# Attention over a graph on one core: one fp32 one-hot in a ring of five batches instead of two, the steps of PE, ScalarE and VectorE in another order, and the node numbers read as long runs

## The chip, the cores and the metric

The kernel runs on one core of a Trainium2 chip. The metric is the device time of one execution in microseconds (us). Before the change the median of three runs is 2317.58 us (2315.75 to 2317.67).

## What is computed

3,125 nodes carry 128 numbers each; 53,125 edges, sorted by their destination node, go from a node `src` to a node `dst`. Four layers follow one another, each with a residual and a layer norm: three sum messages over the edges, and the last is attention over them, in 8 heads of 16 numbers:

```python
q = (h @ Wq + bq).reshape(n, OUT_DIM, H) * scaling
k = (h @ Wk + bk).reshape(n, OUT_DIM, H)
v = (h @ Wv + bv).reshape(n, OUT_DIM, H)
s = jnp.einsum('edh,edh->eh', q[row], k[col])
m = jax.ops.segment_max(s, row, num_segments=n)
p = jnp.exp(s - m[row])
z = jax.ops.segment_sum(p, row, num_segments=n)
out = jax.ops.segment_sum((p / z[row])[:, None, :] * v[col], row, num_segments=n)
```

Here `row` is `src` and `col` is `dst`. The edges come in both directions (each drawn pair twice, and a loop for each node), and the kernel groups edges by `dst` and gathers keys and values by `src`, which gives the same sums.

## The kernel before, in words

The edges are cut into 416 chunks of 128 (one edge for each partition). The three sum layers take up the first 1,640 us or so; GpSimd (POOL) fetches the rows of each chunk with an indirect DMA, VectorE (DVE) makes one-hot factors, TensorE (PE) multiplies. The change touches none of that. It touches two stages behind it.

**The stage between the layers** (`post_body` in `sum_layers`). A loop of 15 turns, `u` = 0 to 14, over pairs of the 25 node tiles. DVE does in each turn `last_front(u)` (bias, residual, statistics), `keys_values(u - 2)`, `last_back(u)` (normalise), and then small tables for the attention: `row_tables` in turns 1 to 7 and `chunk_tables` (line 1165), two in each of the turns 3 to 8 and one in turn 9. `chunk_tables` compares each edge's node with its neighbour's. It reads `dT`, in which partition `c * 8 + head` holds the node numbers of chunk `c` of each of the 26 batches, 130 numbers a batch. POOL loads `dT` with 16 DMAs (line 540), one for each `c`: 26 pieces of 130 numbers, out of the array `flat`, to each of 8 partitions. The first `chunk_tables` waits until all 16 have landed. ScalarE (ACT) turns each pair of tables into penalties (line 788) in its own turns 5 to 12, and the rest behind the loop. SyncE (SP) stores keys and values to memory; when they are there, POOL may begin with the gathers of attention.

**Attention** (`attention`). POOL gathers keys and values of one chunk after another (line 1418, 416 gathers), into a ring of 64 chunks. The others work in batches of 16 chunks; a batch has four parts `q` of 4 chunks. Step `k` of the loop (`STEPS`, -1 to 28) has three batches in work: `k` ("now": its scores), `k-1` ("mid": its maxima and weights), `k-2` ("old": its sums), and prepares `k+1` ("nxt"). In a step each engine has its orders written out by hand, and each engine works them off in that order. The orders that matter:

- PE: `window_sums(q)` (lines 1485 and 1488) is the sum of the weighted values of 4 chunks into a window of 40 nodes: 8 fp32 products of `PV` with the one-hot `S01`, and 8 small ones. `queries(q)` (1448) spreads the queries of a window over 4 chunks of edges. `one_hot_rows(q)` (1438) turns the one-hot over, for the queries of the next batch. `scores_t`, `rows`, `columns`, `weights_back`, `difference` belong to the running maxima and the weights. `output_t` turns over a finished tile of nodes.
- DVE: `products(q)` (1684) multiplies queries with gathered keys: it waits for `queries(q)` and for the gathers. `head_part` (1690) sums them by head. `chunk_max` and `segment_max` scan for the maxima (1701, 1702), `row_max` (1715 to 1722) carries them over the chunks. `values(q)` (1751) weighs the gathered values into `PV`, a ring of two, so that `values(q)` waits until PE is through with `window_sums(q - 2)`. `add(q)` (1778) adds a window's sums. `one_hots(k)` (1677) makes the bf16 one-hot `oh1` of a batch with 4 instructions, and `window_factors(k)` (1738) makes the same one-hot again in fp32, as `S01`, with 4 more. `outputs(t)` and `normalise(t)` finish a tile.
- ACT: `rows_copy`, `rows_ordered`, `columns_copy` (1572 to 1589) move maxima about between PE and DVE. `deviation` (1609) needs its own function table, `weights` (1593, the exponential) another, so each is preceded by a table load. `thrice(q)` (1561) spreads `oh1` for `one_hot_rows(q)`, `one_hot_copy(q)` (1568) takes its result out of PSUM.

25 of the steps have a tile to finish (`outputs`), a few have none.

## Time and profile before

| | |
|---|---|
| median of 3 runs | 2317.58 us |
| the profiled execution | 2318.64 us, with a span of 2316.4 us |
| busy over the span: PE / DVE / ACT / POOL | 70% / 66% / 19% / 71% |
| sum layers | to about 1640 us |
| stage between | 1640 to 1733 us |
| gathers of attention | 1709.6 to 2266.1 us |
| steps of attention | 1735 to 2316 us |

The span is that of the instructions; 2.2 us of the execution lie around it. Matmuls are pipelined and their ends are modelled, so PE's busy share is not a share of its peak. A wait is put down to the last of the events it waited for.

### The profile page before, as it was taken

The numbers are of one execution on the slowest core, as the hardware profiler recorded it, in microseconds if no ns is written. First come the engines' busy times: TensorE is split into PE (matmuls) and PEld (weight loads), VectorE is DVE, ScalarE is ACT, GpSimd is POOL, SyncE is SP. The second block draws the span as 40 slices with busy tenths as digits, with TensorE's granted clock in tenths as the row PEclk, the third lists the DMA queues.
The fourth block names the chain that finished last, engine by engine and source line by source line (L and its number), as shares of the span: only waits on it lengthen the run. The fifth ranks groups of instructions, "written<-read, shape, count | busy, mean of one in ns | idle before, by whom it ended". The sixth has DMA issues, their size and how long they took to land.

```text
span 2316.4 us, 31992 instructions
## 1 busy us (share of the span) xinstructions
PE 1620.7 (70%) x8464; PEld 1228.6 (53%) x8464; DVE 1527.4 (66%) x5213; ACT 430.7 (19%) x906; POOL 1639.1 (71%) x1687
## 2 busy tenths in 40 slices
PE   4877777774767666765576656767547888888886
PEld 3555555553545544544444444444335767777775
DVE  8776766665656665665355555555667787788785
ACT  0000000002000000002011111111154443344342
POOL 6777777775777777775777777776237777777771
PEclk9755555555565666666567777777775555555555
DMA  5233233232233233234223233233444333333330
GB/s 139 56 84 85 56 84 86 56 85 73 55 84 85 84 85 112 57 84 143 67 84 98 84 99 98 84 99 93 67 128 114 108 105 108 109 105 106 108 104 22
DMA packets 149508, 207.34 MB, mean 90 GB/s; under 512 B 48664, under 2 KB 111115, under 8 KB 149216
## 3 DMA queue, kind: packets, MB, share of 16 engines
q0 software_dynamic: 61280, 138.20, 22.4%
q1 hardware_dynamic: 86898, 65.12, 9.4%
q10 hardware_dynamic: 1154, 1.99, 0.3%
q8 instruction: 72, 1.18, 0.2%
q14 instruction: 104, 0.85, 0.1%
HBM read 172.41 MB, written 36.04 MB: 90 GB/s over the span
## 4 chain that ended last, share of the span: by engine, by line
POOL 38%; PE 23%; issue 17%; DVE 10%; DMA 7%; ACT 3%; DVEq 0%; SPq 0%; POOLq 0%; ACTq 0%
POOL G L529 37%; PE p_w L1485 6%; PE p_g L595 4%; DMA G<-h_d,idx 4%; DMA G<-in_x,idx 3%; PE p_oh L1438 2%; PE p_w L1488 2%; PE p_d L606 1%; DVE hs L1690 1%; PE p_d L641 1%; PE p_o L626 1%; DVE XH L1684 1%; ACT oht L1568 1%; DMA agg<-in_flat 1%; ACT ohn L1561 1%
## 5 line engine op out<-in xcount | busy, mean ns | idle before, releaser
L529 POOL DMA_INDIRECT G<-h_d,idx x832 | 794.3, 955 | 283.2 <-issue 259.5
L595 PE MATMUL p_g<-S,G 128*128 128x96 f32 (+1 forms) x2496 | 602.3, 387 | 470.9 <-DMA G<-h_d,idx 286.3
L595 PEld LDWEIGHTS p_g<-S,G 128*128 128x128 f32 x2496 | 521.3, 289 | 670.7 <-DVE S L954 290.7
L1418 POOL DMA_INDIRECT G<-kv_d,idx x416 | 430.2, 1034 | 178.4 <-issue 176.6
L529 POOL DMA_INDIRECT G<-in_x,idx x416 | 402.4, 967 | 132.7 <-issue 119.5
L979 DVE TENSOR_SCALAR work<-iota_h,key_f 128x600 bf16<-128x600 f16 x416 | 169.1, 406 | 257.0 <-PE p_d L606 256.3
L954 DVE SCALAR_TENSOR_TENSOR S<-con,rel,shared 128x96 f32<-128x96 f32 (+1 forms) x1248 | 315.8, 294 | 0.7
L606 PE MATMUL p_d<-work 128*128 128x312 bf16 (+1 forms) x832 | 267.1, 421 | 23.8 <-DVE work L994 22.6
L972 DVE TENSOR_TENSOR agg<-agg,p_g 128x96 f32 (+1 forms) x624 | 144.0, 231 | 113.4 <-PE p_g L595 91.5
L1485 PE MATMUL p_w<-S,PV 128*128 128x40 f32 x832 | 198.4, 414 | 0.7 <-DVE PV L1751 0.7
L994 DVE TENSOR_TENSOR work<-work,p_d 128x312 f32 (+1 forms) x416 | 191.1, 459 | 11.4 <-issue 10.2
L1485 PEld LDWEIGHTS p_w<-S,PV 128*128 128x128 f32 x832 | 185.8, 328 | 15.9 <-issue 10.8
L1070 DVE TENSOR_TENSOR work<-work,p_d 128x512 f32<-128x512 f32 (+1 forms) x168 | 104.3, 625 | 133.5 <-PE p_d L641 133.1
L641 PE MATMUL p_d<-work,q_s 128*128 128x512 bf16 (+1 forms) x525 | 162.1, 432 | 1.9 <-DVE q_s L1059 0.9
L606 PEld LDWEIGHTS p_d<-work 128*128 128x128 bf16 x832 | 116.4, 162 | 40.4 <-DVE work L980 23.9
L1438 PE MATMUL p_oh<-idb,ohn 128*120 128x128 bf16 x416 | 68.9, 321 | 67.7 <-ACT ohn L1561 42.9
L1690 DVE TENSOR_REDUCE hs<-XH 128x32 f32<-128x512 f32 x104 | 111.5, 1072 | 3.6
L745 ACT ACTIVATE xt_s<-p_xt 128x128 f32<-128x128 f32 x75 | 20.8, 277 | 486.1 <-PE p_xt L617 486.1
L980 DVE TENSOR_SCALAR work<-iota_h,lo_f 128x128 bf16<-128x128 f16 x416 | 110.0, 264 | 0.0
L1751 DVE TENSOR_TENSOR PV<-G,ps 128x512 f32<-128x512 f32 x104 | 69.0, 685 | 48.4 <-PE p_w L1488 48.1
L1438 PEld LDWEIGHTS p_oh<-idb,ohn 128*120 128x120 bf16 x416 | 52.0, 214 | 84.4 <-ACT ohn L1561 56.4
L641 PEld LDWEIGHTS p_d<-work,q_s 128*128 128x128 bf16 x525 | 60.5, 124 | 39.2 <-issue 16.1
(250 smaller groups left out, 2038.3 us busy)
## 6 DMA issues: line engine op xcount, KB each, us to landing
work<-A_d SPq DMA_DIRECT2D x25, 800.0 KB, 4.5
A_d<-work SPq DMA_DIRECT2D x12, 1600.0 KB, 7.5
G<-h_d,idx POOLq DMA_INDIRECT x832, 2.5
G<-in_x,idx POOLq DMA_INDIRECT x416, 2.5
G<-kv_d,idx POOLq DMA_INDIRECT x416, 2.7
h_d<-XH SPq DMA_DIRECT2D x75, 64.0 KB
h_d<-in_x SPq DMA_DIRECT2D x2, 1600.0 KB, 7.6
QW<-q_d SPq DMA_DIRECT2D x104, 30.0 KB, 2.0
```

The source lines that it names most:

```text
L529: pool.indirect_dma_start(G[:, c % GRING, :], None, l.table, bass.IndirectOffsetOnAxis(ap=l.places[:, c:c + 1], axis=0)).then_inc(s_arr[g ...
L595: last = pe.matmul(p_g[:, g % PB, 0:width], G[:, c % GRING, :], S[:, c % (SRING * GR), 0:width], start=(k == 0), stop=(k == GR - 1))
L606: last = pe.matmul(p_d[:, 1 + half, 0:(hi - lo) * W], lows[:, slot, :], keys[:, slot, lo * W:hi * W], start=(k == 0), stop=(k == GR - 1))
L641: last = pe.matmul(p_d[:, n % 3, 0:width], q_s[:, t % QS, k, :], A_s[:, t % AB, cols], start=(k == 0), stop=(k == QR - 1))
L954: last = dve.scalar_tensor_tensor(S[:, slot + k, 0:l.nb * W].rearrange("p (b w) -> p b w", w=W), bc(iota, 1, l.nb), rel[:, c:c + 1], bc(co ...
L972: dve.tensor_tensor(place, place, p_g[:, g % PB, 0:l.nb * W].rearrange("p (b w) -> p b w", w=W), ALU.add).then_inc(s_added, 1)
L979: dve.tensor_scalar(keys[:, slot, :], iota_h[:], key_f[:, c:c + 1], None, ALU.is_equal)
L994: dve.tensor_tensor(place, place, p_d[:, 1 + half, 0:(hi - lo) * W].rearrange("p (t w) -> p t w", w=W), ALU.add).then_inc(s_bad, 1)
L1418: pool.indirect_dma_start(G[:, c % KRING, :], None, d["kv"], bass.IndirectOffsetOnAxis(ap=idx[:, c:c + 1], axis=0)).then_inc(s_arr[c // QC ...
L1438: last = pe.matmul(p_oh[0:QR * WA, c * P:(c + 1) * P], ohn[:, k % 2, j * QC + c, :], idb[:], start=True, stop=True)
L1485: pe.matmul(p_w[:, q % 2, 0:WA], PV[:, q % 2, c, :], S01[:, j * QC + c, :], start=(c == 0), stop=(c == QC - 1))
L1690: dve.tensor_reduce(hs[:, j * QC:(j + 1) * QC, :], prod[:, j * QC:(j + 1) * QC, :].rearrange("p c (d h) -> p c h d", h=HEADS), AX_X, ALU.a ...
```

## The change

Nothing of the computation changes. The parts:

1. The one-hot of a batch is made once, in fp32, in a ring of five batches (`oh1`, `OH1 = 5`). PE uses it for the window sums in place of `S01`; ACT's `thrice` reads it in place of the bf16 one. `window_factors`, its semaphore and `S01` are gone. DVE makes the one-hot of batch `k+2` in step `k`, where it was `k+1`; DVE has a step -2 for that. A slot is free again when the sums of its batch are done.
2. `PV` has three buffers where it had two (`VRING = 3`).
3. PE does `scores_t` and `queries(4k)` between the first two `window_sums`, and `queries(4k+2)` ahead of `columns`. DVE does `products(4k)` ahead of `chunk_max`. ACT does two `thrice` at the very start of a step and the other two ahead of the first `one_hot_copy` and of `weights`.
4. The node numbers come in an array `runs`, laid out on the host as each `c`'s 26 x 130 numbers in one run, so each of the 16 DMAs reads one contiguous run of 3,380 numbers a partition.
5. `chunk_tables` moves from turns 3 to 9 to turns 6 to 12 on DVE, and on ACT to two in each of the turns 7 to 12.
6. Three small tiles (`ot`, `y`, `o_s`) lie in unused columns of another tile.

```diff
-                first = 0 if c < CB - 1 else 2
-                runs = a["flat"][first:EP + first].rearrange("(k x) -> k x", x=CB * P)
-                pool.dma_start(dT[c * HEADS:(c + 1) * HEADS],
-                               runs[:, c * P - first:(c + 1) * P + 2 - first].partition_broadcast(HEADS)
-                               ).then_inc(s_dT, 16)
+                pool.dma_start(dT_flat[c * HEADS:(c + 1) * HEADS], a["runs"][c].partition_broadcast(HEADS)).then_inc(s_dT, 16)
...
-                if 0 <= u - 5 < KB // 2:
-                    chunk_tables(u - 5)
-            for n in range(DUOS - 5, KB // 2):
+                for n in (2 * u - 14, 2 * u - 13):
+                    if u >= 7:
+                        chunk_tables(n)
+            for n in range(2 * DUOS - 14, KB // 2):
                 chunk_tables(n)
...
-                if 3 <= u <= 8:
-                    chunk_tables(2 * u - 6)
-                    chunk_tables(2 * u - 5)
-                if u == 9:
+                if 6 <= u <= 11:
+                    chunk_tables(2 * u - 12)
+                    chunk_tables(2 * u - 11)
+                if u == 12:
                     chunk_tables(12)
...
-    oh1 = sb("oh1", [P, 2, CB, WA], BF16)
+    oh1 = sb("oh1", [P, OH1, CB, WA])
...
-    S01 = sb("S01", [P, CB, WA])
-    PV = sb("PV", [P, 2, QC, D])
+    PV = sb("PV", [P, VRING, QC, D])
...
                 if old:
                     window_sums(4 * k - 8)
-                    window_sums(4 * k - 7)
                 if mid:
                     scores_t(k - 1)
                 if now:
                     queries(4 * k)
+                if old:
+                    window_sums(4 * k - 7)
+                if now:
                     queries(4 * k + 1)
                 if mid:
                     rows(k - 1)
                 if old:
                     window_sums(4 * k - 6)
+                if now:
+                    queries(4 * k + 2)
                 if mid:
                     columns(k - 1)
-                if now:
-                    queries(4 * k + 2)
...
                 mid, nxt = batch(k - 1), batch(k + 1)
+                if nxt:
+                    thrice(4 * k + 4)
+                    thrice(4 * k + 5)
                 if mid:
                     penalties(k - 1)
...
                 if nxt:
-                    thrice(4 * k + 4)
-                    thrice(4 * k + 5)
+                    thrice(4 * k + 6)
+                    thrice(4 * k + 7)
                     one_hot_copy(4 * k + 4)
                 if mid:
                     weights(k - 1)
                 if nxt:
-                    thrice(4 * k + 6)
-                    thrice(4 * k + 7)
                     one_hot_copy(4 * k + 5)
...
         def one_hots(k):
-            if k >= 2:
-                dve.wait_ge(s_ohn, 4 * (k - 1))
+            if k >= OH1:
+                dve.wait_ge(s_mm, 4 * (k - OH1 + 1))
+                dve.wait_ge(s_ohn, 4 * (k - OH1 + 1))
...
-            if q >= 2:
-                dve.wait_ge(s_mm, q - 1)
-            dve.tensor_tensor(PV[:, q % 2].rearrange("p c (d h) -> p c d h", h=HEADS),
+            if q >= VRING:
+                dve.wait_ge(s_mm, q - VRING + 1)
+            dve.tensor_tensor(PV[:, q % VRING].rearrange("p c (d h) -> p c d h", h=HEADS),
...
                     add(4 * k - 8)
+                if now:
+                    products(4 * k, landed)
                 if mid:
                     chunk_max(k - 1)
                 if now:
-                    products(4 * k, landed)
                     head_part(4 * k)
...
-                if nxt:
-                    one_hots(k + 1)
+                if batch(k + 2):
+                    one_hots(k + 2)
...
                 if mid:
-                    window_factors(k - 1)
                     if k > 1:
```

## Rows read from the trace of the kernel before

**Rows 1.** Stretches, us: busy PE, PEld, DVE, ACT, POOL; PE clock, DMA share, GB/s.

```profile
1826.11:1847.76 21.65, 17.98 (x114) 15.49 (x114) 17.62 (x47) 9.35 (x21) 16.78 (x17) 0.50 0.37 104
...
1955.29:1974.15 18.86, 17.73 (x115) 15.30 (x114) 15.69 (x39) 7.20 (x19) 14.43 (x14) 0.50 0.37 106
```

**Rows 2.** Timeline of one step: start, length, instruction, and the idle time before it.

```profile
1995.74 1.93 PE L1485 MATMUL p_w<-S,PV 128*128 128x40 f32 x8
...
1998.40 0.69 DVE L1751 TENSOR_TENSOR PV<-G,ps 128x512 f32<-128x512 f32 x1 [2.15 <-PE p_w L1488]
...
2000.99 1.06 PE L1448 MATMUL p_qe<-QW,oht 120*128 120x128 bf16 x8
...
2006.60 0.58 PE L1459 MATMUL p_sm<-con,R 1*128 1x1 f32 x2 [1.07 <-ACT R L1584]
```

**Rows 3.** Timeline of ACT and PE in the second half of that step.

```profile
2007.65 0.17 ACT L1589 ACTIVATE ic<-p_sm 128x2 f32<-128x2 f32 x1 [1.10 <-PE p_sm L1460]
...
2009.34 1.08 ACT L1561 ACTIVATE ohn<-oh 128x480 bf16<-128x480 bf16 x2
2010.69 0.60 ACT L1568 ACTIVATE oht<-p_oh 120x512 bf16<-120x512 f32 x1 [0.28 <-PE p_oh L1438]
...
2012.60 0.31 ACT L1593 ACTIVATE pT<-Dt 128x128 f32<-128x128 f32 x1
...
2009.97 0.68 PE L1438 MATMUL p_oh<-idb,ohn 128*120 128x128 bf16 x4 [1.82 <-ACT ohn L1561]
...
2013.36 0.42 PE L1476 MATMUL p_bk<-con,pT 128*128 128x128 f32 x1
...
2017.40 0.86 PE L1485 MATMUL p_w<-S,PV 128*128 128x40 f32 x3
```

**Rows 4.** Timeline of POOL: the gathers around two of DVE's stretches.

```profile
1993.74 1.30 POOL L1418 DMA_INDIRECT G<-kv_d,idx  x1 [0.30 <-issue]
...
2006.60 2.10 POOL L1418 DMA_INDIRECT G<-kv_d,idx  x1 [0.30 <-issue]
```

**Rows 5.** Timeline of DVE at those gathers.

```profile
1992.94 1.28 DVE L1751 TENSOR_TENSOR PV<-G,ps 128x512 f32<-128x512 f32 x2
...
2006.11 1.01 DVE L1677 TENSOR_TENSOR oh<-con,rel 128x160 bf16<-128x160 f32 x4
...
2007.20 0.67 DVE L1751 TENSOR_TENSOR PV<-G,ps 128x512 f32<-128x512 f32 x1
```

**Rows 6.** POOL's first gather, number 48 and the last one (timeline).

```profile
1709.59 1.05 POOL L1418 DMA_INDIRECT G<-kv_d,idx  x1 [51.99 <-issue]
...
1771.64 0.94 POOL L1418 DMA_INDIRECT G<-kv_d,idx  x1 [0.30 <-issue]
...
2265.20 0.94 POOL L1418 DMA_INDIRECT G<-kv_d,idx  x1 [0.30 <-issue]
```

**Rows 7.** POOL in the stretch from gather 48 to gather 96.

```profile
1771.64:1834.28 62.64, 48.02 (x49) 0.50 0.39 109
```

**Rows 8.** The last `products` of attention on DVE (timeline).

```profile
2274.66 0.69 DVE L1684 TENSOR_TENSOR XH<-p_qe,G 128x512 f32<-128x512 f32 x1
```

**Rows 9.** The stage between: the node numbers' DMAs, and DVE's wait (timeline).

```profile
1647.34 10.26 POOL L540 DMA_DIRECT2D agg<-in_flat  x16 [1.57 <-issue]
...
1671.00 0.77 DVE L1165 TENSOR_TENSOR shared<-agg 128x258 f32<-128x258 int32 x2 [12.40 <-DMA agg<-in_flat]
...
1674.79 0.74 DVE L1165 TENSOR_TENSOR shared<-agg 128x258 f32<-128x258 int32 x2
```

**Rows 10.** A stretch of the stage between; DMA issues (KB each, us to landing).

```profile
1656.00:1660.00 4.00, 2.54 (x14) 1.68 (x12) 2.42 (x9) 1.85 (x6) 1.60 (x3) 1.00 1.10 83
...
work<-A_d SPq DMA_DIRECT2D x25, 800.0 KB, 4.5
...
G<-kv_d,idx POOLq DMA_INDIRECT x416, 2.7
```

More of the change, by code:

```diff
@@ L67 @@
 QRING = 8
+OH1 = 5
+VRING = 3
 OR = 3
@@ L325, in sum_layers @@
     pick = agg[0:NSTEP, 3, 0:NSTEP // 4 * P]
-    dT = agg[:].rearrange("p b n -> p (b n)")[:, 2 * AGW:2 * AGW + KB * (P + 2)].bitcast(I32).rearrange("p (k e) -> p k e", k=KB)
+    dT_flat = agg[:].rearrange("p b n -> p (b n)")[:, 2 * AGW:2 * AGW + KB * (P + 2)].bitcast(I32)
+    dT = dT_flat.rearrange("p (k e) -> p k e", k=KB)
     ends = agg[0:1, 0, 0:2 * (EC + 1)].bitcast(I32).rearrange("p (b c) -> p b c", b=2)
@@ L1316, in attention @@
     al = sb("al", [P, 2])
-    S01 = sb("S01", [P, CB, WA])
-    PV = sb("PV", [P, 2, QC, D])
+    PV = sb("PV", [P, VRING, QC, D])
     zt = sb("zt", [P, 2, HEADS])
     zr = sb("zr", [P, 2, HEADS])
-    ot = sb("ot", [P, 2, D])
-    y = sb("y2", [P, 2, D])
+    ot = XH[:, NT + CB:NT + CB + 2]
+    y = XH[:, NT + CB + 2:NT + CB + 4]
     bn6 = sb("bn62", [P, 2, 6])
@@ L1326, in attention @@
     rstd = sb("rstd2", [P, 2, 1])
-    o_s = sb("o_s", [P, OR, D])
+    o_s = XH[:, NT + CB + 4:NT + CB + 4 + OR]
     p_oh = psum("p_oh", [P, QC * P])
@@ L1341, in attention @@
         sem(f"a_{k}") for k in ("fb", "rows", "r0", "pen", "scan", "carry", "r2", "cols", "ic", "fb2", "m", "d"))
-    s_ex, s_bk, s_ps, s_df, s_a1, s_al, s_rsc, s_s01, s_pv, s_mm, s_add = (
-        sem(f"a_{k}") for k in ("ex", "bk", "ps", "df", "a1", "al", "rsc", "s01", "pv", "mm", "add"))
+    s_ex, s_bk, s_ps, s_df, s_a1, s_al, s_rsc, s_pv, s_mm, s_add = (
+        sem(f"a_{k}") for k in ("ex", "bk", "ps", "df", "a1", "al", "rsc", "pv", "mm", "add"))
     s_z1, s_z2, s_ot, s_po, s_y, s_bs, s_ba, s_std, s_rs, s_done = (
@@ L1365, in attention @@
     STEPS = range(-1, KB + 3)
+    DVE_STEPS = range(-2, KB + 3)
     def passes(eng, ns, turn, body):
@@ L1480, in window_sums @@
             pe.wait_ge(s_pv, q + 1)
-            pe.wait_ge(s_s01, q + 1)
+            pe.wait_ge(s_oh1, q + 1)
             if q >= 2:
@@ L1484, in window_sums @@
             for c in range(QC):
-                pe.matmul(p_w[:, q % 2, 0:WA], PV[:, q % 2, c, :], S01[:, j * QC + c, :], start=(c == 0),
+                pe.matmul(p_w[:, q % 2, 0:WA], PV[:, q % VRING, c, :], oh1[:, k % OH1, j * QC + c, :], start=(c == 0),
                           stop=(c == QC - 1))
@@ L1488, in window_sums @@
                 last = pe.matmul(p_w[0:HEADS, q % 2, WA:2 * WA], ps[:, k % 2, j * QC + c, :],
-                                 S01[:, j * QC + c, :], start=(c == 0), stop=(c == QC - 1))
+                                 oh1[:, k % OH1, j * QC + c, :], start=(c == 0), stop=(c == QC - 1))
             last.then_inc(s_mm, 1)
@@ L1561, in thrice @@
             act.activation(ohn[:, k % 2, chunks].rearrange("p c (w s) -> p c w s", s=QR),
-                           bc(oh1[:, k % 2, chunks], 3, QR), ACT.Copy).then_inc(s_ohn, 1)
+                           bc(oh1[:, k % OH1, chunks], 3, QR), ACT.Copy).then_inc(s_ohn, 1)
         def one_hot_copy(q):
@@ L1672, in one_hots @@
         def one_hots(k):
-            if k >= 2:
-                dve.wait_ge(s_ohn, 4 * (k - 1))
+            if k >= OH1:
+                dve.wait_ge(s_mm, 4 * (k - OH1 + 1))
+                dve.wait_ge(s_ohn, 4 * (k - OH1 + 1))
             for j in range(4):
                 c = k * CB + j * QC
-                dve.tensor_tensor(oh1[:, k % 2, j * QC:(j + 1) * QC, :], bc(iota, 1, QC),
+                dve.tensor_tensor(oh1[:, k % OH1, j * QC:(j + 1) * QC, :], bc(iota, 1, QC),
                                   bc(rel[:, c:c + QC], 2, WA), ALU.is_equal).then_inc(s_oh1, 1)
@@ L1731, in segment_max @@
             dve.tensor_tensor(Dt[:], p_sT[:, 0:P], M[:, k % 2, :], ALU.subtract).then_inc(s_d, 1)
-        def window_factors(k):
-            if k > 0:
-                dve.wait_ge(s_mm, 4 * k)
-            for j in range(4):
-                c = k * CB + j * QC
-                dve.tensor_tensor(S01[:, j * QC:(j + 1) * QC, :], bc(iota, 1, QC), bc(rel[:, c:c + QC], 2, WA),
-                                  ALU.is_equal).then_inc(s_s01, 1)
         def fade_log(k):
@@ L1811, in vector @@
             sweep_start()
-            for k in STEPS:
+            for k in DVE_STEPS:
                 now, mid, old, nxt = batch(k), batch(k - 1), batch(k - 2), batch(k + 1)
@@ L1890, in layout @@
         "last4": f(ends[1::2, -1]),
-        "flat": flat,
+        "runs": f(flat[np.arange(EC)[:, None] * P + np.arange(P + 2)].reshape(KB, CB, P + 2).transpose(1, 0, 2)
+                  ).reshape(CB, KB * (P + 2)),
         "clast": f(flat[0::P]),
```

## The prediction

> **What bounds the kernel now.** I read the stretches first. In attention an ordinary step, which finishes a tile, takes 21.65 us, and one without a tile 18.86. PE is busy 17.98 of the 21.65, DVE 17.62, POOL 16.78, ACT 9.35, and PE's granted clock is 0.50, its lower level of 1.2 GHz, throughout [rows 1]. No engine is full by that count. The timeline of one step shows why the step is no shorter. PE waits 1.07 us before `columns` [rows 2] and 1.82 before the first `one_hot_rows`, since ACT's `thrice` comes late [rows 3]. DVE waits 2.15 before `values(4k-6)` for the second buffer of `PV` [rows 2]. So PE's order sets the step, with waits inside it.
>
> POOL hides a second bound. Behind every gather stand 0.30 us of issue, so a gather of 0.95 takes 1.25, and 16 of them 20.0 us, which is the least a step can average. It isn't reached. Two gathers a step are longer: 2.10 and 1.30 us [rows 4]. Set them against DVE [rows 5]: the one at 2006.60 ends at 2008.70, 0.83 behind the end of `values` at 2007.87; the one at 1993.74 ends at 1995.04, 0.82 behind the end of the pair of `values` at 1994.22. No gather waits for a free place in the ring: by count that gather is number 224 or close to it, and number 256 would be the first that needs `values` of that moment. A gather that starts while DVE is in its run of `one_hots` and `values` is held until the run is over. The run lasts from 2006.11 to 2007.87.
>
> The Trainium skill, page "SBUF — State Buffer", section on the shared port, says that a VectorE instruction with two SBUF inputs and a GpSimd instruction that reads SBUF exclude each other for the whole instruction. The trace agrees at `values` (two SBUF inputs). It agrees less at `window_factors`, of the same kind. I come back to that among the rivals.
>
> In the stage between, the chain of waits goes through the node numbers: POOL issues 16 DMAs from 1647.34 to 1657.60, and DVE stands still for 12.40 us, until 1671.00 [rows 9].
>
> **Part by part, the stage between.** The first `chunk_tables` moves from turn 3 to turn 6. A turn takes 3.79 us (1671.00 to 1674.79), 0.74 of it the two tables [rows 9], so 3.05 without. DVE reaches the place of the wait at 1671.00 - 12.40 = 1658.60; three turns on is 1667.8. The numbers landed at 1671.0, over a DMA system that was full (share 1.10, 83 GB/s) [rows 10]. The runs carry the same 16 x 105.6 KB, 1.69 MB, in pieces of 13.5 KB instead of 520 bytes. A load with long pieces moved 800 KB in 4.5 us, 178 GB/s [rows 10]. At that rate 1.69 MB take 9.5 us, less than POOL's issue of 10.26, so they land soon after 1660 and nobody waits. Bounds: if the long pieces are no faster, turn 6 waits 1671.0 - 1667.8 = 3.2 us. The moved tables cost the same 13 instructions on DVE. The last pair delays one `keys_values` by 0.4 us, which PE's work on the queries covers. ACT's tables move into turns where it idles. I take the whole 12.4 us, bounds 9.2 and 12.4. The gathers start that much earlier too, since POOL waits for the stored keys and values, which hang on the same turns.
>
> **Attention, the step.** DVE loses 4 instructions a step, `window_factors`, which make the same as `one_hots`, 1.01 us for four [rows 5]. That is off the path as long as PE or POOL sets the step. The fp32 one-hot costs what `window_factors` cost, and PE's products keep their shapes. What counts is the order on PE. Before, `columns` came at 2006.60 - 1995.74 = 10.86 us into the step, of which 1.07 were its wait; so 9.8 us of work stood before it. One more `queries` does now, 0.53 us (two took 1.06) [rows 2]: PE reaches `columns` at 9.8 + 0.5 = 10.3, if its input is there. By DVE's new order it should be: DVE no longer stands 2.15 us in front of `values`, and `row_max` comes about 1.5 us earlier than before. That last number is an estimate from the wait that goes, less what DVE then waits for `queries(4k)`.
>
> From `columns` to ACT's copy is 1.05 us (2006.60 to 2007.65), and from that copy to the end of the two `thrice` 2.77 (2010.42); `one_hot_copy` to the end of the exponential takes 2.22 (2010.69 to 2012.91) [rows 2, 3]. The sum is 10.3 + 1.05 + 2.77 + 2.22 = 16.3 us; before it was 17.17. But before, PE came to `weights_back` only at 2013.36, 17.62 into the step, because of the 1.82 us lost ahead of `one_hot_rows`. That wait goes, since two `thrice` now stand at the start of the step, on a one-hot made a step earlier. PE would be there at about 15.2, and waits for the exponential until 16.3. From there to the next step are 2017.40 - 2013.36 = 4.04 us [rows 3]. New step by this chain: 16.3 + 4.0 = 20.3 us, 1.3 less. Bounds: nothing gained (21.65), and 15.2 + 4.0 = 19.2 if ACT is quicker than I reckon.
>
> **Attention, the gathers.** At 20.3 us a step the gathers can't follow. From gather 48 to gather 96 the steps were short (18 to 19 us), so POOL was alone in its pace: 62.64 us for 48 gathers, 20.88 for 16 [rows 7]. The ends are 20.0 (nothing held up) and 21.65 (as much as before). I take 20.88, as it was measured with DVE's instructions running at full density. The first 48 take 1771.64 - 1709.59 = 62.05 us [rows 6], the remaining 367 to the start of the last one 367 / 16 x 20.88 = 478.9, together 541.0. Before it was 2265.20 - 1709.59 = 555.6 [rows 6]. That is 14.6 us. POOL also had a lead: the last gather started at 2265.20 and is used by `products` at 2274.66 [rows 8]; with 0.94 for itself and 2.7 to land [rows 10], 5.8 us are spare, and they are used up now. Behind the last `products` one `window_sums` fewer stands before `scores_t`, and the chain through `columns` gains about 1 us. Sum: 14.6 + 5.8 + 1.0 = 21.4 us. The chain alone would give 1.3 x 23 steps = 30, so the gathers decide: DVE's `products` will wait for them late in attention, and the third buffer of `PV` and the missing `window_factors` only make that wait longer.
>
> Against the profiled execution (2318.64): 2318.64 - 12.4 - 21.4 = 2284.8. The median lies 1.06 lower, so I predict 2284 us.
>
> **Rivals.**
> 1. *The step stays as it was, only the stage between gains.* If ACT's row of table load, `thrice`, copy, table load ends no earlier, for instance since `rows` slips behind the second `window_sums`, the step stays at 21.65: 2317.6 - 12.4 - 1.0 = 2304. For it: the exponential gains only 0.9 us on the path, so a small slip upstream eats it. Against it: PE's wait of 1.82 us goes anyway.
> 2. *The gathers go faster than 20.88.* `window_factors` (some 1.0 us) and the pair of `values` (1.28) were one run of DVE; now 1.28 is left [rows 5]. If that run held POOL as the other does, 16 gathers come to nearly 20.0, and the chain of 20.3 decides: (20.88 - 20.3) x 23 = 13 us less, 2271. The rows speak against it: the gather that started at 1993.74 lost only 0.35.
> By the rule of exclusion in the Trainium skill's page "SBUF — State Buffer" this rival would be the likely one, because `window_factors` has two SBUF inputs as well.
> 3. *The runs come late.* If a run of 8 partitions keeps fewer DMA engines busy and all land 6 us later than before, at 1677, turn 6 waits 9 us: 2293. Against it: the full DMA system of rows 10 was full of small pieces.
> 4. *Slower.* DVE does `products(4k)` before `chunk_max`, and PE holds `columns` until after `queries(4k+2)`, which needs products too. Each us by which `columns` comes later than now passes whole through ACT's row into the step, about 25 times. To lose the 13.4 us of the rest, the step must grow by 0.54, so `columns` has to start at about 12.2 into the step or later, not at 10.3. At 12.8 the step is 22.8: 2317.6 - 13.4 + 1.15 x 25 = 2333. DVE's waits of 2.15 us that fall away speak against it.
>
> **How the numbers follow.** The forecast, 2277 to 2292, gets 0.48. Rival 1, with what lies between it and the forecast, gets 0.24, rival 2 0.14, rival 3 0.06, rival 4 0.05, and an end where one gain is cancelled by a small loss elsewhere (no change) 0.03. Range: from rival 2's 2271 to a little beyond rival 1's 2304, so 2270 to 2305. A measurement of this kernel can tell some 0.2%, 4.6 us. Faster by more than that: 0.92; within: 0.03; slower: 0.05.
>
> **What would show it.** Right: no wait of DVE ahead of its first `chunk_tables`; the first gather near 1697; steps of 20.3 to 21 us; the wait ahead of the first `one_hot_rows` gone, and one ahead of `weights_back` in its place; from gather 48 on 20.7 to 21 us for 16; late in attention DVE waiting for gathers ahead of `products`. Wrong: gathers at 21.65 per 16 as before (rival 1), a wait of PE for ACT's copy ahead of `columns` (rival 4), or a granted clock that rises to its upper level of 2.4 GHz, which would shorten PE's pieces and leave the gathers as the only bound.

## The result, and the profile after

| | before | changed |
|---|---|---|
| median, us (4 runs each, same chip) | 2317.62 (2315.75 to 2319.12) | 2301.97 (2296.58 to 2304.62) |
| ratio | | 0.9931 [0.9919, 0.9942] |
| profiled execution: time / span, us | 2318.64 / 2316.4 | 2304.62 / 2302.7 |

The change saved 15.6 us, 0.69%. The forecast was 33.6 us. In the profiled executions, between which the span fell by 13.7, I cut the time in three. Up to the stage between the layers (the first product of `w_lin`) the changed kernel is 2.2 us later, which is spread from run to run. From there to the first gather it takes 63.0 us where before took 66.0: 3.0 gained, 12.4 forecast. From the first gather to the end it takes 593.9 us where before took 606.8: 12.9 gained, 21.4 forecast. Both halves fell short, and each by a cause of its own. These are two single executions. In all the profiles taken on an ordinary chip the stage lasts 66.0 to 67.6 us in its old form (three kernels) and 60.4 to 63.6 in the changed form (six), so the 3.0 is at the low end of what the stage gains.

**The stage between.** First the timeline of the changed kernel, PE, POOL, SP's queue and DVE picked out of it: start, length, instruction, idle time before it.

```profile
1645.80 1.15 PE L675 MATMUL p_g<-w_lin,work 128*128 128x128 f32 x8 [1.75 <-DVEq L1249]
...
1647.85 4.99 POOL L541 DMA_DIRECT2D agg<-in_runs  x10
1653.75 3.00 POOL L541 DMA_DIRECT2D agg<-in_runs  x6 [0.91 <-issue]
...
1655.84 0.39 SPq L503 DMA_DIRECT2D kv_d<-kv_s  x1
...
1675.88 0.69 DVE L1204 TENSOR_TENSOR kv_s<-p_d,b_all 128x512 f32<-128x512 f32 x1 [10.59 <-DMA kv_d<-kv_s]
...
1680.86 0.75 DVE L1165 TENSOR_TENSOR shared<-agg 128x258 f32<-128x258 int32 x2
...
1708.80 1.03 POOL L1418 DMA_INDIRECT G<-kv_d,idx  x1 [52.05 <-issue]
```

The wait ahead of the tables (12.40 us in [rows 9]) is gone, as forecast. In its place DVE stands still for 10.59 us in front of `keys_values`, which writes into a place of the ring `kv_s` (three places) whose last content is not stored yet. That store was issued at 1655.84, among the last of the runs. The DMA view of the same stretch (1646 to 1682) has, for each queue, packets, MB and share of 16 engines, and for each issue the median time to landing:

```profile
q0 software_dynamic: 608, 1.76, 35.5%
q1 hardware_dynamic: 1360, 1.31, 12.3%
...
agg<-in_runs POOLq DMA_DIRECT2D x16, 105.6 KB, 5.0
kv_d<-kv_s SPq DMA_DIRECT2D x5, 256.0 KB, 14.1
```

A median hides what matters here. Of the five stores, the three that were issued while the runs were under way took 14.1, 16.9 and 19.9 us, the two behind them 2.1. The runs spread as widely: the first ones land after 3 us, and of those issued between 1655 and 1657 the same trace has (minimum, median, maximum)

```profile
DMA to landing us min/median/max: 11.6/15.7/19.4
```

So the last of the node numbers, issued at 1656.24, land at 1675.6, and the store of 1655.84 at 1675.8. The numbers come later than in the kernel before (1671.0), not soon after 1660 as forecast: 1.69 MB in 27.8 us are 61 GB/s, and the prediction had reckoned with 178. Without its wait for the store DVE would have been at the first `chunk_tables` at 1680.86 - 10.59 = 1670.3 and would have waited some 5 us there (an estimate). While the runs move, the DMA engines are little more than half busy (the last three numbers are PE clock, DMA share and GB/s; the share before was 1.10 in [rows 10]):

```profile
1660.00:1670.00 10.00, 4.03 (x20) 2.75 (x20) 4.94 (x19) 2.98 (x8) 0.00 (x0) 1.00 0.57 97
```

**Attention.** Of the page, POOL's gathers and DVE's `products` (busy, mean ns, idle before):

```profile
L1418 POOL DMA_INDIRECT G<-kv_d,idx x416 | 424.2, 1020 | 178.6 <-issue 177.9
...
L1688 DVE TENSOR_TENSOR XH<-p_qe,G 128x512 f32<-128x512 f32 x104 | 71.2, 685 | 77.8 <-DMA G<-kv_d,idx 64.8
```

and `products` between 1780 and 2240 alone, by what its engine waited for (us, times):

```profile
  DMA G<-kv_d,idx: 58.1, 39
```

In the kernel before there is no such wait in this window. At first the changed kernel runs as forecast. In the step that begins at 1882.25 `columns` starts 10.1 us into it (10.3 forecast) and `weights_back` 16.1 (16.3). Of the 25 intervals between two `weights_back` two are short (17.0 and 17.6 us) and the next seven take 20.2. Then the gathers' lead is used up, and but for the last ones, which are short again, the steps lie between 20.2 and 22.7. PE's timeline shows the turn, with intervals of 20.20, 18.50 (a step that has no tile to finish) and 22.66:

```profile
1918.55 0.48 PE L1476 MATMUL p_bk<-con,pT 128*128 128x128 f32 x1 [0.88 <-ACT pT L1595]
1938.75 0.48 PE L1476 MATMUL p_bk<-con,pT 128*128 128x128 f32 x1 [0.88 <-ACT pT L1595]
1957.25 0.42 PE L1476 MATMUL p_bk<-con,pT 128*128 128x128 f32 x1
1979.91 0.48 PE L1476 MATMUL p_bk<-con,pT 128*128 128x128 f32 x1 [0.88 <-ACT pT L1595]
```

The gathers' own pace answers to [rows 6]:

```profile
1772.16 0.95 POOL L1418 DMA_INDIRECT G<-kv_d,idx  x1 [0.30 <-issue]
...
2258.15 1.34 POOL L1418 DMA_INDIRECT G<-kv_d,idx  x1 [0.30 <-issue]
```

The first 48 took 63.36 us (62.05 before), and the other 367 took 485.99 us, 21.19 for 16. In the kernel before the same 367 took 493.56 us by [rows 6], 21.52 for 16. What makes a gather long is seen when POOL's timeline is laid beside DVE's. First POOL, from one late step:

```profile
2013.03 0.95 POOL L1418 DMA_INDIRECT G<-kv_d,idx  x1 [0.30 <-issue]
...
2015.53 1.83 POOL L1418 DMA_INDIRECT G<-kv_d,idx  x1 [0.30 <-issue]
...
2029.39 1.36 POOL L1418 DMA_INDIRECT G<-kv_d,idx  x1 [0.30 <-issue]
```

and DVE:

```profile
2015.52 1.01 DVE L1681 TENSOR_TENSOR oh<-con,rel 128x160 f32<-128x160 f32 x4
...
2027.21 0.69 DVE L1688 TENSOR_TENSOR XH<-p_qe,G 128x512 f32<-128x512 f32 x1 [2.10 <-DMA G<-kv_d,idx]
...
2029.25 0.68 DVE L1747 TENSOR_TENSOR PV<-G,ps 128x512 f32<-128x512 f32 x1
...
2032.79 0.69 DVE L1688 TENSOR_TENSOR XH<-p_qe,G 128x512 f32<-128x512 f32 x1 [2.35 <-DMA G<-kv_d,idx]
```

The gather of 2015.53 ends at 2017.36, 0.83 behind the end of the four `one_hots` (2016.53). The one of 2029.39 ends at 2030.75, 0.82 behind `values` (2029.93). An undisturbed one lasts 0.95. I went through all 416 gathers this way: 62 last more than 1.08 us and lose 28.2 us together, counted above 0.95. Before it was 54 of them and 34.3 us, but there the gathers had a lead and nobody waited. Sorted by the instruction that DVE had begun last when the gather started, some 9 us of the 28 were lost at `one_hots` (or the small copies right ahead of it) and some 17.6 at `values` (or the `add` right ahead of it). The same trace has the counterpart: 42 gathers start within a `values`, which reads two operands in SBUF, and 31 of them last more than 1.08 us; 44 start within a `products` of the same length, which reads one operand in PSUM, and none of them lasts more than 0.96.

### The profile page after: what moved, and what is told of

Same layout as the page of the kernel before. It is cut to its first block, busy times and chain, and to the rows that moved or that the text cites. A ratio compares the mean times of both kernels' runs of the same rounds, so it can differ in the third digit from the quotient of the medians.

```text
span 2302.7 us, 31884 instructions
## 1 busy us (share of the span) xinstructions
PE 1626.5 (71%) x8440; PEld 1233.5 (54%) x8464; DVE 1501.0 (65%) x5109; ACT 430.7 (19%) x906; POOL 1632.2 (71%) x1687
## 3 DMA queue, kind: packets, MB, share of 16 engines
q0 software_dynamic: 60512, 138.18, 22.3%
## 4 chain that ended last, share of the span: by engine, by line
POOL 55%; issue 20%; PE 11%; DMA 8%; DVE 5%; ACT 1%; DVEq 0%; POOLq 0%; ACTq 0%; SPq 0%
POOL G L532 39%; POOL G L1418 17%; PE p_g L594 4%; DMA G<-in_x,idx 3%; DMA G<-h_d,idx 3%; PE p_d L605 1%; DMA kv_d<-kv_s 1%; PE p_o L625 1%; PE p_d L640 1%; PE p_w L1485 1%; DMA G<-kv_d,idx 0%; DVE work L1010 0%; DVE work L994 0%; DVE S L954 0%; PE p_o L626 0%
## 5 line engine op out<-in xcount | busy, mean ns | idle before, releaser
L594 PE MATMUL p_g<-S,G 128*128 128x96 f32 (+1 forms) x2496 | 610.4, 391 | 469.9 <-DMA G<-h_d,idx 315.9
L594 PEld LDWEIGHTS p_g<-S,G 128*128 128x128 f32 x2496 | 527.7, 293 | 673.5 <-issue 315.1
L1418 POOL DMA_INDIRECT G<-kv_d,idx x416 | 424.2, 1020 | 178.6 <-issue 177.9
L605 PE MATMUL p_d<-work 128*128 128x312 bf16 (+1 forms) x832 | 272.8, 429 | 19.9 <-DVE work L994 18.9
L1485 PE MATMUL p_w<-oh,PV 128*128 128x40 f32 x832 | 197.8, 413 | 0.1
L1485 PEld LDWEIGHTS p_w<-oh,PV 128*128 128x128 f32 x832 | 187.7, 331 | 11.9 <-issue 10.8
L640 PE MATMUL p_d<-work,q_s 128*128 128x512 bf16 (+1 forms) x501 | 148.3, 414 | 6.7 <-issue 4.1
L1688 DVE TENSOR_TENSOR XH<-p_qe,G 128x512 f32<-128x512 f32 x104 | 71.2, 685 | 77.8 <-DMA G<-kv_d,idx 64.8
L744 ACT ACTIVATE xt_s<-p_xt 128x128 f32<-128x128 f32 x75 | 20.8, 278 | 494.8 <-PE p_xt L616 494.8
L1438 PEld LDWEIGHTS p_oh<-idb,ohn 128*120 128x120 bf16 x416 | 52.2, 214 | 50.5 <-issue 26.5
```

The lines of the kernel that those rows point to most:

```text
L594: last = pe.matmul(p_g[:, g % PB, 0:width], G[:, c % GRING, :], S[:, c % (SRING * GR), 0:width], start=(k == 0), stop=(k == GR - 1))
L605: last = pe.matmul(p_d[:, 1 + half, 0:(hi - lo) * W], lows[:, slot, :], keys[:, slot, lo * W:hi * W], start=(k == 0), stop=(k == GR - 1))
L640: last = pe.matmul(p_d[:, n % 3, 0:width], q_s[:, t % QS, k, :], A_s[:, t % AB, cols], start=(k == 0), stop=(k == QR - 1))
L1418: pool.indirect_dma_start(G[:, c % KRING, :], None, d["kv"], bass.IndirectOffsetOnAxis(ap=idx[:, c:c + 1], axis=0)).then_inc(s_arr[c // QC ...
L1438: last = pe.matmul(p_oh[0:QR * WA, c * P:(c + 1) * P], ohn[:, k % 2, j * QC + c, :], idb[:], start=True, stop=True)
L1485: pe.matmul(p_w[:, q % 2, 0:WA], PV[:, q % VRING, c, :], oh1[:, k % OH1, j * QC + c, :], start=(c == 0), stop=(c == QC - 1))
```

## The experiments

Theory for the stage: the runs' DMAs (8 partitions each) hold the stores up, and the wait has only moved; rival: the tables' new place is at fault. Theory A for attention: compares with two operands in SBUF hold gathers, and the gathers set the late steps; rivals: the gathers' pace is their own, or the chain of PE and ACT is slower than forecast.

**The stage, four kernels on another chip.** On that chip the kernel before takes 2967.3 us and these four 2964 to 2988, with idle time in all engines throughout attention; so only the stage between is read there. The attention of the change doesn't pay on that chip: s2 (old stage, new attention) takes 1.0061 [1.0041, 1.0081] of the kernel before, clearly more, and s1 (new stage, old attention) 0.9990 [0.9968, 1.0011]. Why isn't shown, and what the text says of attention holds for the ordinary chip. The two waits of the stage of 12.40 and 10.59 us come back as 12.63 and 10.29.

`s1_stage_only`: the kernel before with the runs and the moved tables. Its diff is the change's parts around lines 326, 535, 813 and 1229, at the core:

```diff
-                if 3 <= u <= 8:
-                    chunk_tables(2 * u - 6)
-                    chunk_tables(2 * u - 5)
-                if u == 9:
+                if 6 <= u <= 11:
+                    chunk_tables(2 * u - 12)
+                    chunk_tables(2 * u - 11)
+                if u == 12:
                     chunk_tables(12)
```

> The kernel before with only the parts of the stage between: the node numbers as long runs, and chunk_tables in turns 6 to 12. Attention is as before. Theory (the wait only changed its place): DVE no longer waits for the numbers ahead of chunk_tables, but 9 to 12 us ahead of keys_values in turn 5, since the store of the slot that it needs is stuck behind the runs. The first gather comes 1 to 4 us earlier, counted from the first matmul of the stage; the time is 1 to 4 us under before, about 2315. Rival (the two halves of the change disturb each other, each alone is worth its forecast): 12 us under before, 2305.

`s2_attention_only`: the changed kernel with these parts undone (the same diff, taken back).

> The changed kernel with the stage between as before: old pieces of node numbers, chunk_tables in turns 3 to 9. Theory (the gathers bound attention): 11 to 15 us under before, about 2305, DVE's wait of 12.4 us ahead of chunk_tables is back, the time from the first gather to the end is 593 to 596 us as in the changed kernel. Rival (attention gains less by itself, since the stage's new order feeds it): under 8 us.

`s3_old_pieces_moved_tables`: the changed kernel, tables in their new turns, node numbers in pieces of 520 bytes.

```diff
-                pool.dma_start(dT_flat[c * HEADS:(c + 1) * HEADS], a["runs"][c].partition_broadcast(HEADS)).then_inc(s_dT, 16)
+                first = 0 if c < CB - 1 else 2
+                runs = a["flat"][first:EP + first].rearrange("(k x) -> k x", x=CB * P)
+                pool.dma_start(dT[c * HEADS:(c + 1) * HEADS],
+                               runs[:, c * P - first:(c + 1) * P + 2 - first].partition_broadcast(HEADS)
+                               ).then_inc(s_dT, 16)
```

> The changed kernel with the node numbers in the old pieces of 520 bytes; chunk_tables stay moved. Theory (a store shares its DMA engines with long runs and waits behind them, behind short pieces it gets its turn sooner: 13.8 us at most in before, against some 20): the wait ahead of keys_values in turn 5 shrinks from 10.6 to 2 to 5 us, DVE may wait another 0 to 3 ahead of chunk_tables in turn 6; 3 to 7 us faster than the changed kernel. Rival (only the bytes in front of the store count): the wait stays at 9 to 12 us and the time equals the changed kernel's.

`s4_one_dma`: the changed kernel, all node numbers in one DMA; the array lies in memory once for each of the 128 partitions.

```diff
-            for c in range(CB):
-                pool.dma_start(dT_flat[c * HEADS:(c + 1) * HEADS], a["runs"][c].partition_broadcast(HEADS)).then_inc(s_dT, 16)
+            pool.dma_start(dT_flat, a["runs"]).then_inc(s_dT, 16)
...
-                  ).reshape(CB, KB * (P + 2)),
+                  ).reshape(CB, KB * (P + 2)).repeat(HEADS, 0),
```

> The changed kernel with the node numbers in one DMA of 128 partitions, in place of 16 DMAs of 8 partitions each (the array holds each run 8 times over). Theory (a DMA of 8 partitions keeps only about half of the DMA engines at work, and its long runs block them): the 1.7 MB land within about 10 us of their issue, by 1660, the stores wait less than 2 us, the wait in turn 5 is 0 to 1 us; 8 to 11 us faster than the changed kernel, 2291 to 2294. Rival (the receiving side or the sum of bytes is the limit): the numbers land no earlier than before, the wait in turn 5 stays at 8 us or more.

| kernel | first product to first gather, us | DVE's wait for DMA | first product to landing of the last node number, us | node numbers' queue, share of 16 engines | stores issued before the numbers had landed, us to landing |
|---|---|---|---|---|---|
| s2 (stage as before) | 66.2 | 12.63, tables | 27.6 | 51.2% | 10.4 to 14.1 |
| s1 (stage as changed) | 62.9 | 10.29, `keys_values` | 29.7 | 35.1% | 13.7 to 19.6 |
| s3 | 57.6 | 3.80 and 1.06, `keys_values` | 27.6 | 51.3% | 7.2 to 14.1 |
| s4 | 52.2 | none | 10.6 | 16.1% | 2.1 |

The rows behind the table's waits, of s1, s3 and s2, each a row of DVE's timeline:

```profile
2109.43 0.69 DVE L1202 TENSOR_TENSOR kv_s<-p_d,b_all 128x512 f32<-128x512 f32 x1 [10.29 <-DMA kv_d<-kv_s]
```

```profile
2114.24 0.69 DVE L1208 TENSOR_TENSOR kv_s<-p_d,b_all 128x512 f32<-128x512 f32 x1 [3.80 <-DMA kv_d<-kv_s]
```

```profile
2112.85 0.77 DVE L1168 TENSOR_TENSOR shared<-agg 128x258 f32<-128x258 int32 x2 [12.63 <-DMA agg<-in_flat]
```

The waits are as expected in all four. The same node numbers (1.76 to 1.78 MB in the queue) take 51, 35 or 16% of the DMA engines' time in 36 us. The lower share of the long runs is no relief for DVE: they land 2 us later than the small pieces, and the first store lands with them, after 19.6 us (10.4 in s3). Moving the tables alone (s3) is worth 8.6 us; together with the long runs only 3.3. In one DMA onto 128 partitions the node numbers land 8.6 us after issue, and nobody waits: 14.0 us less than in s2, the forecast 12.4 and a little more. How busy the DMA engines are meanwhile is seen in s1, s3 and s4 (the last three numbers: PE clock, DMA share, GB/s):

```profile
2084.00:2104.00 20.00, 10.44 (x48) 7.11 (x47) 13.31 (x49) 7.33 (x20) 5.54 (x12) 0.93 0.56 89
```

```profile
2094.00:2110.00 16.00, 9.21 (x45) 6.77 (x45) 13.87 (x50) 6.55 (x18) 6.30 (x11) 0.93 1.06 110
```

```profile
2087.00:2091.00 4.00, 3.91 (x14) 3.15 (x15) 2.99 (x11) 1.45 (x5) 0.00 (x0) 0.50 0.86 302
```

That the late numbers and the late stores make the wait is shown. Why the runs are slow is shown only in part. Their 128 packets of 13,520 bytes are in work eight at a time nearly throughout in the changed kernel, and most take 1.6 us, the last ones 1.3 to 1.4; in s4 the same packets go sixteen at a time, and most take 0.5 us. The Trainium skill, page "DMA: Bandwidth & Descriptors", section "Why a DMA increments its semaphore by 16 and not by 1", says that a DMA is spread over as many engines, at most 16, as divide the outermost dimension of both sides. That gives 8 engines for 8 partitions, and 16 for s4. The eight and sixteen packets at a time agree with it. It leaves two things open. The small pieces of s3 go to 8 partitions as well, and there the engines are full (1.06). And a packet of the runs takes about three times as long as in s4. There s4 differs in one thing more: each partition reads numbers of its own in memory, while 8 partitions read the same run in the changed kernel. No run changes one of these two without the other.

**Attention, on an ordinary chip** (before: 2318.43 us median). `t1_iota_in_psum`: one operand of `one_hots` moves.

```diff
+    iota_p = p_sT[:, 400:400 + WA]
...
+        dve.tensor_copy(iota_p, iota)
...
-                dve.tensor_tensor(oh1[:, k % OH1, j * QC:(j + 1) * QC, :], bc(iota, 1, QC),
+                dve.tensor_tensor(oh1[:, k % OH1, j * QC:(j + 1) * QC, :], bc(iota_p, 1, QC),
                                   bc(rel[:, c:c + QC], 2, WA), ALU.is_equal).then_inc(s_oh1, 1)
```

> One part changed against the changed kernel: the node numbers 0 to 39 that one_hots compares with are copied once to free columns of PSUM bank p_sT and read from there, so that these four instructions a step have one operand in SBUF instead of two. Theory A (a gather that starts while VectorE runs an instruction with two operands in SBUF is held until about 0.83 us after that instruction's end, and the changed kernel's 21.19 us per 16 gathers over the forecast 20.88 come from such meetings): one_hots no longer holds a gather, 16 gathers take 20.4 to 20.8 us, the time falls by 8 to 16 us against the changed kernel. Rival B (the gathers' pace is their own and VectorE's instructions have no part in it): 21.1 to 21.3 us per 16, time within 2 us of the changed kernel. Rival C (the step is set by the chain of products, weights and sums, and the gathers are held up by it): VectorE's read from PSUM is no faster, no change or some us slower.

Measured: 2279.63 us (2279.09 to 2280.08), 0.9835 [0.9817, 0.9852]; 22.3 us less than the changed kernel, where theory A had 8 to 16. The page:

```profile
L1419 POOL DMA_INDIRECT G<-kv_d,idx x416 | 402.0, 966 | 179.0 <-issue 179.0
...
L1690 DVE TENSOR_TENSOR XH<-p_qe,G 128x512 f32<-128x512 f32 x104 | 71.0, 683 | 19.7 <-PE p_qe L1449 19.5
```

POOL's busy time falls from 424.2 to 402.0, by 22.2 us, and the time by as much. DVE's wait for gathers is gone. Counted as above, 22 gathers are long and lose 5.8 us, and from the 48th on 16 gathers take 20.30 us (20.4 to 20.8 expected). The 22 that start within `one_hots` last 0.95 each, so the 9 us lost there are gone. The larger part of the gain is at `values`, which still reads two operands in SBUF: it cost 17.6 us and costs some 4 now. In steps of an even 20.2 us fewer long gathers meet it (8 in place of 31). I take that for a matter of rhythm, which theory A had not priced; no run tests it by itself. The compares take as long as before (1.00 us for four). DVE and POOL, side by side, at the next `one_hots`:

```profile
2026.27 1.00 DVE L1683 TENSOR_TENSOR oh<-p_sT,rel 128x160 f32<-128x160 f32 x4
```

```profile
2025.38 1.05 POOL L1419 DMA_INDIRECT G<-kv_d,idx  x1 [0.30 <-issue]
2026.74 0.95 POOL L1419 DMA_INDIRECT G<-kv_d,idx  x1 [0.30 <-issue]
```

The gather of 2026.74 starts in the middle of the compares and lasts 0.95. Theory A holds in its mechanism, though its size was too small; rivals B and C fall. The trace agrees with the rule that the prediction quoted (the Trainium skill, "SBUF — State Buffer", section "Who interferes with whom", on two SBUF inputs). It adds that the held gather ends 0.83 us behind DVE's instruction.

`t2_half_the_gathers`: every odd chunk comes by a plain DMA of fixed rows.

```diff
+                if c % 2 == 1:
+                    at = c % (NT - 1) * P
+                    pool.dma_start(G[:, c % KRING, :], d["kv"][at:at + P, :]).then_inc(s_arr[c // QC % KQ], 16)
+                    continue
```

> In the changed kernel every second gather of attention becomes a plain DMA of 128 fixed rows of the same table, as many bytes into the same place with the same signal: the output is not the reference's, the number of scores, products and sums is. It takes GpSimd's cost of a gather down and leaves the chain of the other engines as it is. If the step by the chain alone is the 20.3 us that the prediction has, 16 batches of 16 chunks take 20.2 to 20.5 us each and the time falls by 18 to 26 us against the changed kernel. If the chain is itself what sets 21.2 us a step, the time stays within 3 us. If VectorE, which waits 58 us of 460 for gathers, takes the step over at its busy time plus its other waits, the step is 19 to 20 us and the time falls by 30 us or more.

The output is not that of the attention here, only its work is. POOL now has time to spare; of its idle time, most is for a free place in the ring:

```profile
L1422 POOL DMA_INDIRECT G<-kv_d,idx x208 | 213.5, 1026 | 213.8 <-DVE PV L1751 113.9
```

Measured: 2282.38 us (2 runs), and 20.2 us in 20 of the 25 intervals between two `weights_back`; the others are the short ones. So the chain alone makes 20.2, and the forecast 20.3 was right. t1 has the same 20 intervals of 20.2: there the gathers are just quick enough.

`t3_three_more_compares` and `u4_four_compares_back` put compares back where `window_factors` stood. In `t3` there are three, 128 elements each (`WM` is 32):

```diff
+        def more_factors(k):
+            for j in range(3):
+                c = k * CB + j * QC
+                dve.tensor_tensor((more_b if j < 2 else more_a)[:, j % 2], bc(iota[:, 0:WM], 1, QC),
+                                  bc(rel[:, c:c + QC], 2, WM), ALU.is_equal)
...
                 if mid:
+                    more_factors(k - 1)
```

> The changed kernel with three more instructions a step like those that the change took out of this place (a compare of two operands in SBUF, 128 elements a partition, some 0.8 us each, written to unused space, nobody waits for them). VectorE was idle about 3 us a step, most of it waiting for gathers, so its time alone has room for them. Theory A (each such instruction holds a gather that meets it): 16 gathers take 0.6 to 1.2 us more, the time rises by 15 to 30 us, most of what the change gained in attention. Rival B (the removal only gave VectorE time that it did not need): rise of 0 to 5 us.

Measured: 2297.55 us (2 runs), 4.4 less than the changed kernel and within its spread. The expectation had taken the length of a whole run of four for that of one; they last 0.28 us each. So `u4` has four of 160 elements, with output in bf16, 1.0 us together:

```diff
+            for j in range(4):
+                c = k * CB + j * QC
+                dve.tensor_tensor(more_b[:, j] if j < 3 else more_a[:], bc(iota, 1, QC),
+                                  bc(rel[:, c:c + QC], 2, WA), ALU.is_equal)
```

> The changed kernel with four compares a step where window_factors stood, of its operands and size (both in SBUF, 1.0 us for four), into unused space; nobody waits for them. The run with three smaller ones showed that they last 0.2 us each and not 0.8 as expected there, 0.6 us a step, and no loss. Theory A: what decides is whether a gather starts in such a run of VectorE; 1.0 us right ahead of the pair of values makes one run of 2.3 us, and the time rises by 4 to 12 us. Theory B: the place falls between starts of gathers as often as not and VectorE's wait for gathers takes it up: within 3 us, and the removal of window_factors had no part in the gain of 15.6 us.

Measured: ratio 0.9929 [0.9904, 0.9954] to before, where the changed kernel has 0.9931. DVE waits less for gathers, 44.2 us in the window where it waited 58.1, and works more. Theory B holds as far as the time goes: putting such compares back costs nothing that these runs can tell (the interval is 5.8 us to either side). The compares do hold gathers, though. In u4, 18 gathers start within them, end 0.81 to 0.82 us behind the end of the one compare in which they started, and lose 1.8 us together; in the kernel before it was 21 gathers at `window_factors`, none longer than 1.02, with 1.2 us together. So the rule of two operands in SBUF holds at `window_factors` as well, where the prediction saw it agree less. The difference is that a gather is held there until the end of one compare, and at `one_hots` often to the end of the whole run of DVE: in the kernel before, 22 gathers that start within `one_hots` lose 22.4 us. Why the two places differ is open.

`t4_one_dma_and_iota`: s4 and t1 together.

> The changed kernel with both edits: all node numbers loaded by one DMA onto 128 partitions (instead of 16 of 8 partitions), and the compare's node numbers 0 to 39 in PSUM as in the run before. Theory: the stage between the layers takes 52 to 54 us from its first product to the first gather (63.0 in the changed kernel), and with theory A of the gathers 16 of them take 20.4 to 20.8 us: together 2280 to 2286 us where the kernel before takes 2317.6. If only the stage gains, 2291 to 2294 us. If neither, 2302.

Measured: 2268.06 us (2267.70 to 2268.59), 0.9784 [0.9767, 0.9802]: 50.4 us under before, 33.9 under the changed kernel, and 12 under the lower end of what was expected, since attention again gains more than theory A had (20.30 us for 16 gathers). The stage takes 52.4 us (1641.00 to 1693.43), and no DVE wait for a DMA is left in it. This is the fastest version.

**The halves alone, and a last control** (before: 2321.78 us median). `u1_stage_alone` is s1's kernel and `u2_attention_alone` s2's, now on an ordinary chip.

> The kernel before with the change's first half alone (node numbers in long runs, the tables moved three turns). Expected from the two traces: VectorE's 12.40 us ahead of the tables go, and 7 to 11 us ahead of the sum of keys and values come in their place; the first gather starts 2 to 6 us earlier after the stage's first product than the 65.95 us of before, and attention is unchanged: 2312 to 2316 us, a ratio of 0.9975 to 0.999 to the kernel before. If the prediction's 12.4 us were there after all: 2305, ratio 0.9947.

Measured: 2315.07, ratio 0.9975 [0.9964, 0.9987], with a wait of 9.71 us ahead of `keys_values`.

> The changed kernel with the stage between the layers as it was before. Expected from the two traces: 66 us to the first gather as before, and attention 12 to 14 us shorter: 2303 to 2307 us, ratio 0.9935 to 0.9955. If the two halves depend on each other (gathers that start earlier need fewer stalls later), the two gains of this run and the one before do not add up to the 15.6 us of the whole change.

Measured: 2306.12, ratio 0.9932 [0.9909, 0.9954]. The two halves give 0.25% and 0.68% (5.8 and 15.8 us), together 0.93%; the whole change gave 0.69%. The intervals (some 0.12 and 0.22 points to either side) leave room for both readings, so whether the halves depend on each other stays open.

`u3_before_with_iota_in_psum` is the kernel before with t1's edit, in both places that compare:

```diff
-                dve.tensor_tensor(S01[:, j * QC:(j + 1) * QC, :], bc(iota, 1, QC), bc(rel[:, c:c + QC], 2, WA),
+                dve.tensor_tensor(S01[:, j * QC:(j + 1) * QC, :], bc(iota_p, 1, QC), bc(rel[:, c:c + QC], 2, WA),
                                   ALU.is_equal).then_inc(s_s01, 1)
```

> The kernel before with the compare's node numbers 0 to 39 read from PSUM, in one_hots and in window_factors, nothing else changed. Theory: in the kernel before the step is set by the order of the products on PE and its waits (21.65 us), and a gather that is held costs nothing as long as the gathers have a lead; so the gathers are held less and the step stays at 21.6 to 21.7: the time falls by 0 to 4 us, though the same edit took 22 us from the changed kernel. Rival: the gathers set the pace of the kernel before as well; then it falls by 10 us or more.

Measured: ratio 0.9995 [0.9985, 1.0005]. POOL's busy time fell all the same, from 430.2 to 405.3 us, and the last gather started at 2243.18 instead of 2265.20. The steps stayed at 21.65:

```profile
2014.26 0.42 PE L1477 MATMUL p_bk<-con,pT 128*128 128x128 f32 x1
2035.91 0.42 PE L1477 MATMUL p_bk<-con,pT 128*128 128x128 f32 x1
```

The same edit is worth nothing in the kernel before and 22 us in the changed one. That is the plainest sign of what the change did: it took the chain from 21.65 to 20.2, and made the gathers the bound. (The gathers of before, 21.52 us for 16, were close to it already.)

## Why the prediction was right and where it failed

- *Direction, and the range of 2270 to 2305*: right. *The time*: 18 us too low, for two steps that failed.
- *The numbers land soon after 1660 (1.69 MB at 178 GB/s, 9.5 us), nobody waits, and all 12.4 us of the tables' wait are gained*: this failed first. The last numbers landed at 1675.6, 27.8 us after the first issue, at 61 GB/s and later than before; the rate had been taken from a load of another shape. The stores of keys and values issued beside them took 14.1 to 19.9 us, so DVE met the late stores one turn before it would have met the late numbers, and waited 10.59 us ahead of `keys_values`. Gained: 3.0 us in the two profiles, 5.8 us (0.25%, interval 3.0 to 8.4) by u1. The lower bound of 9.2 supposed that the long pieces are no slower than the small ones, and no bound was made for what else is under way in the same stretch. In s4, where the numbers land after 8.6 us and the stores in 2.1, the step gives 14.0.
- *Rival 3 (a run of 8 partitions keeps fewer DMA engines busy, and the numbers come late, at 1677)*: its mechanism is borne out, at 1675.6 and with a DMA share of 0.57 where the small pieces had 1.10; and a stall of its size (9 us) came, 10.59. What it lacked is that the stores would be late as well and that DVE would meet them first. It had a chance of 0.06.
- *The step by the chain, 20.3 us*: right, 20.2 in seven early steps, and in all ordinary ones of t2 and t1, and right term by term (10.1, 16.1 and 20.2 for 10.3, 16.3 and 20.3). The wait ahead of the first `one_hot_rows` went, and one ahead of `weights_back` (0.88 us) came, as forecast.
- *The gathers, not the chain, decide; late in attention DVE waits for them*: right, 58.1 us of waits, none before; t1 and u3 show it.
- *16 gathers in 20.88 us*: mis-sized, 21.19 measured, and the first 48 took 63.36 us and not 62.05. These two make 7.1 + 1.3 = 8.4 of the 8.5 us that attention lacks. The prediction called its row (gathers 48 to 96) a stretch of short steps; by the trace only the steps up to 1800 were short, from there on to 1834 they took 21.8 and 21.65. Over all the 367 gathers [rows 6] gives 21.52. How many gathers meet a compare or a `values` depends on how the two rhythms fall, and no row of before gave it for steps of 20.3.
- *The first gather near 1697*: it came at 1708.80, by the step on the stage.
- *Rival 2 (without `window_factors` the gathers come near 20.0, 2271)*: wrong, 21.19 with them gone, and u4 puts such compares back without a loss that shows. The pace that it named is nearly reached when `one_hots` stops holding gathers, in t1 (20.30): 2279.63 with the stage as it is, and 11.6 us less with s4's DMA.
- *Rival 1 (only the stage gains, 2304)*: the time is near, by chance; the stage gained least.
- *Rival 4 (`columns` later, slower)*: wrong. PE's waits ahead of `columns` for ACT's copy are 1.5 us in all of attention, where they were 25.6.

## What to carry to other kernels

When a wait for a transfer is taken away, look at every other transfer of that stretch and at the ring that hangs on it: the next wait may be as long, and it was, within 2 us. Take the rate of a transfer from one of the same shape, and read when its last part lands and not the median: here the median was 5.0 us and the last 19.4. When a chain is made shorter, price the engine that fed it with a lead by the pace that it has at the new rhythm, and keep that price as a range. A compare against a constant can read the constant from PSUM; where GpSimd's gathers set the pace, that was worth 22 us of 2302 here, part of it by the rhythm of the steps, and where they didn't, nothing.

## What the runs showed of the hardware that I had not expected

- An operand in PSUM instead of SBUF cost the compare nothing (1.00 us for four against 1.01) and freed the gathers.
- A gather that starts within the compares or `values` ends 0.82 to 0.83 us behind the end of a DVE instruction or of a whole run of them. The most that one lost was 0.99 us in the changed kernel and 1.17 before, where `one_hots` and `values` made one run of 1.76. At `window_factors` 21 gathers lost 1.2 us together.
- The changed kernel's four runs span 8.0 us (2296.58 to 2304.62), the four of t1 1.0 and the four of t4 0.9. That held gathers make the time uneven would fit, but isn't shown: the two runs of t2, where gathers don't set the pace, lie 6.8 apart.
- 1.69 MB of node numbers as one DMA onto 128 partitions landed in 8.7 us, with the stores beside it in 2.1 (t4). As 16 DMAs onto 8 partitions each, with long pieces, the last landed 27.8 us after the first issue, and the stores beside them took 14.1 to 19.9.
